# A fused attention and expert layer: peak products in blocks of three, local scores and values in one group, and the norm among the global heads

## The chip, the cores and the metric

The kernel runs on one core of a Trainium2 chip. The time is the device time of one execution in microseconds (us), smaller is better. The engines have short names in the profile: PE is TensorE (PEld its weight loads), DVE is VectorE, ACT is ScalarE, POOL is GpSimd, and SP is SyncE, which issues the DMAs here. Each runs its own queue in order and waits on semaphores.

## The reference

Tokens are 8 sequences of 1024 with 256 features. After a layer norm, two branches are added to the input:

```python
xn = _layernorm(x)                     # over 256 features
# attention: 16 heads of 16, the first 4 global (causal), 12 local (causal, window 64)
scores = einsum('bhqd,bhkd->bhqk', q, k) * 16 ** -0.5
w = softmax(where(mask, -inf, scores)); ctx = einsum('bhqk,bhkd->bhqd', w, v)
attn = ctx @ w_out + b_out
# experts, forward and inverse: 8 experts of rank 64, K side summed over the tokens so far
prod = einsum('btd,kdr->btkr', Q, V) * cumsum(einsum('btd,kdr->btkr', K, W), axis=1)
weights = softmax(gelu(Q @ router_w1.T + b1) @ router_w2.T + b2 + expert_bias)
out = (einsum('btkr,kdr->btd', prod * weights[..., None], U) + weights @ b) / n_valid
x = x + attn + (fwd + alpha * inv) @ W_O.T
```

The kernel works on 512 tokens at a time.

## The kernel before

The 8192 tokens are cut into 16 chunks of 512, two to a sequence. Of a sequence, the first chunk (even number) has few keys before it, and the second (odd number) has all of the first chunk's. One list of stages, written by the planning code at the top of `mixer_layer`, is walked by all five engines: each engine does its own part of a stage and skips the rest. The order of that list is therefore the order of every queue. `weave(main, side)` runs the groups of `main` one by one and puts the groups of `side` evenly between them.

A chunk has three stretches.

1. **Peaks.** Softmax needs the maximum of the scores of every token and head. The products for these maxima are made first: 12 local peaks (`lpeak`, L780, one PSUM bank each, 64-row halves of the PE array) and then the global peaks (`gpeak`, L794, full array), 10 in an even chunk and 26 in an odd one. Each peak fills one of the banks 5, 6 and 7 in turn, and DVE reduces it to a maximum (L1254, L1261). A bank that holds masked scores has to hold the mask first. For the first three local peaks PE writes it (L774), for the other nine, and for the peaks on the diagonal of the global heads, ACT does (`seed`, L1056 and L1058), and PE waits for `seeded`. Between the peaks stand the groups of the experts: `x` (six products of L639 from XH and XL, copied by ACT at L1040, multiplied by a weight on POOL at L1501), `c` (six products of L639 from CH and CL) with `product` (DVE multiplies at L1334, ACT copies the high part to PH at L1050, POOL makes the rest PL at L1506), `mix` (twelve products of L760) and `open` (four products of L727). A chunk has 21 such groups: product 0, c1, open, mix 0, and then x, c, mix in turn.
2. **Local heads.** Six units, each with scores (`lscore`, L814 and L820, exponentials at L1077) and products with the values (`lav`, L841), with the next chunk's transposes (`turn`, L657) and query and key products (`parts`) between them.
3. **Global heads.** Scores (`gscore`, L855), exponentials (L1085), masks on POOL (L1494) and products with the values (`gav`, L873), with the next chunk's router (`gates`, `gate_parts`), then `cout` (PE transposes, DVE divides at L1344 and L1346), `cparts` (L894, L1100, L1353) and `finish` (L904, L1364), which also ends the chunk's output.

The layer norm of a chunk's tokens (`norm`, nine pieces on DVE, L1174 to L1194) is spread over the peaks stretch of the chunk before it. Its tokens are loaded by `load` (L1547) in the local heads' stretch before that.

`peak_groups` gives the peaks in pairs, and it puts the `seed` of a peak behind the peak two places before it, so that on ACT it stands right behind the preceding pair:

```python
        for n, ((stage, *key),) in enumerate(order + gpeaks):
            if stage is add_lpeak and n > 2:
                order[n - 2].append((add_seed, key[-1], "lpeak", *key[:-1]))
```

Of the kernel before, what the change touches and what calls it, by code (L numbers as in the profile page):

```python
# [41 lines left out]
class Plan:  # L42
# [6 lines left out]
    def add(self, kind, *key, uses=()):  # L49
        self.stages.append((kind, *key))  # L50
        self.count[kind] = self.count.get(kind, 0) + 1
        self.place[(kind, *key)] = self.count[kind]
        self.claim((kind, *key), uses)
# [16 lines left out]
def mixer_layer(  # L70
# [4 lines left out]
    KE, _, R = V_fwd.shape  # L75
# [11 lines left out]
    CHUNKS = NB * NC  # L87
# [2 lines left out]
    HALF = C // 2  # L90
    HE_SLOTS = 6
    WIDE = 3
    assert DB == 2 and NC == 2 and KR == 512 and NG == 4 and NL % 4 == 0 and C // WINDOW == 8

    COL_Q, COL_K, COL_V = 0, D, 2 * D
# [17 lines left out]
    add, nth, use = plan.add, plan.nth, plan.use  # L113
# [21 lines left out]
    def peak_use():  # L135
        turns["peak"] += 1
        return f"bank{(5, 6, 7)[turns['peak'] % 3]}"

    NORM = ("moments", "start", "square", "correct", "square", "correct", "square", "correct", "scale")
# [34 lines left out]
    def add_hidden(ch, j):  # L174
        add_on("hidden", ch, j, uses=[f"bank{2 + j % 2}", exp_use()])

    def add_cout(ch, grp):
        add("cout", ch, grp, uses=["bank4", f"craw{grp % 2}"])
# [13 lines left out]
    def add_lav(ch, grp, half):  # L192
        add("lav", ch, grp, half, uses=["bank7"] if half == 0 else [])
        where["lav", ch, grp, half] = [where["lscore", ch, grp, half, pair][1] for pair in range(2)]
        if half == 1:
            add("cin", ch, grp)
# [10 lines left out]
    def weave(main, side):  # L207

        done = 0
        for n, group in enumerate(main):  # L210
            run(group)
            upto = -(-len(side) * (n + 1) // len(main))
            for other in side[done:upto]:
                run(other)
            done = upto

    def run(group):
        for stage, *key in group:
            stage(*key)

    def local_groups(ch):

        units = [(grp, half) for grp in range(1, 1 + NL // 4) for half in range(2)]
        order = []
        for n, (grp, half) in enumerate(units):
            order.append([(add_lscore, ch, grp, half, pair) for pair in range(2)])
            if n:
                order.append([(add_lav, ch, *units[n - 1])])
            if n > 2 and half:
                order[-1].append((add_cout, ch, grp - 1))  # L230
        return order

    def global_groups(ch):
        order = []
        tl = tiles(ch % NC)
        for n, (j, half) in enumerate(tl):
            order.append([(add_gscore, ch, j, half, pair) for pair in range(2)])
            if n:
                order.append([(add_gav, ch, *tl[n - 1])])
        return order + [[(add_gav, ch, *tl[-1])]]  # L240

    def expert_groups(ch):

        order = []
        for j in range(2 * KB):
            if j < 2 * KB - 1 and (j > 1 or not ch):
                order.append([(add_x, ch, j + 1, part) for part in range(2)] + [(add_weigh, ch, j + 1)])
            order.append([(add_c, ch, j, part) for part in range(2)] if j else [])
            order[-1].append((add_product, ch, j))
            if j == 1 and ch:  # L250
                order.append([(add_open, ch)])
            if j:
                order.append([(add_mix, ch, j - 1, part) for part in range(2)])
        return order
# [4 lines left out]
    def add_residual(ch):  # L259
        add("residual", ch)  # L260
# [7 lines left out]
    def add_weigh(ch, j):  # L268

        add("weigh", ch, j)  # L270
        if j + WIDE < 2 * KB:
            add_wide(ch, j + WIDE)

    def add_wide(ch, j):
        add("wide", ch, j, uses=[f"wide{j % WIDE}"])

    def add_gate_parts(ch):
        add("gate_parts", ch)
        for j in range(WIDE):
            add_wide(ch, j)  # L280
# [4 lines left out]
    def add_rows(ch, which):  # L285
        add("rows", ch, which, uses=["bank4"])

    def peak_groups(ch):
        c = ch % NC
        order = [[(add_lpeak, ch, t, grp, peak_use())] for t in range(T) for grp in range(NL // 4)]  # L290
        gpeaks = [[(add_gpeak, ch, t, j, peak_use())] for t in range(T) for j in range(c * T + t + 1)]
        for n, ((stage, *key),) in enumerate(order + gpeaks):
            if stage is add_lpeak and n > 2:
                order[n - 2].append((add_seed, key[-1], "lpeak", *key[:-1]))
            elif stage is add_gpeak and key[2] == c * T + key[1]:
                (order + gpeaks)[n - 2].append((add_seed, key[-1], "gpeak", *key[:-1]))
        order[-1].append((add, "found", ch, 0))
        gpeaks[2].append((add_rows, ch, 0))
        gpeaks[-1].append((add, "found", ch, 1))
        order += gpeaks  # L300
        if ch + 1 < CHUNKS:
            at_ = len(order) // 3
            step = (len(order) - at_) // len(NORM)
            for n in range(len(NORM)):
                order[at_ + n * step].append((add, "norm", ch + 1, n))
        return [order[n] + (order[n + 1] if n + 1 < len(order) else []) for n in range(0, len(order), 2)]


    add("boot")
# [54 lines left out]
    for ch in range(CHUNKS):  # L364
        nxt = ch + 1 < CHUNKS

        experts, peaks = expert_groups(ch), peak_groups(ch)
        split = len(experts) if nxt else 18
        weave(experts[:split], peaks)
        if ch:  # L370
            add_residual(ch)

        last_mix = [(add_mix, ch, 2 * KB - 1, part) for part in range(2)]
        if nxt:
            side = [[(add_turn, ch + 1, 0)], last_mix, [(add_turn, ch + 1, 1)], [(add, "sums", ch + 1, 0), (add_rows, ch, 1)]]
            side += [[(add_parts, ch + 1, 1, 0), (add, "sums", ch + 1, 1)]]
            side += [[(add_parts, ch + 1, w, b)] for w, b in ((1, 1), (0, 0), (0, 1))]
            if ch + 2 < CHUNKS:
                side[-1].append((add, "load", ch + 2))
        else:  # L380
            side = [[(add_rows, ch, 1)]] + experts[split:] + [last_mix]
        weave(local_groups(ch), side)
        add_lav(ch, NL // 4, 1)
        if nxt:
            add("keep", ch + 1)
            add("stacks", ch + 1, "local")
            add_hidden(ch + 1, 0)
            add_hidden(ch + 1, 1)
        add_cout(ch, NL // 4)
        if nxt:  # L390
            add_hidden(ch + 1, 2)
            add_hidden(ch + 1, 3)

        order = global_groups(ch)
        side = []
        if nxt:
            first_x, first_c = ([(add, ch + 1, 0, part) for part in range(2)] for add in (add_x, add_c))
            run(first_x + order[0] + first_c)
            add("logits", ch + 1, uses=["bank7", "craw0"])
            order = order[1:]  # L400
            side = [[(add_gates, ch + 1)], [(add_gate_parts, ch + 1)]] + [[]] * (2 * (ch % NC))
            side += [[(add_values, ch + 1, 0)], [(add_values, ch + 1, 1)]]
        weave(order, side)
        if nxt:
            add("stacks", ch + 1, "global")
            add("weight_rows", ch + 1, uses=["bank7"])
        add_cout(ch, 0)
        if nxt:
            add_weigh(ch + 1, 0)
            run([(add_x, ch + 1, 1, part) for part in range(2)])  # L410
            add_weigh(ch + 1, 1)
        for k in range(DB):
            add_on("cparts", ch, k, uses=[score_use()])
        if nxt:
            run([(add_x, ch + 1, 2, part) for part in range(2)])
            add_weigh(ch + 1, 2)
        add_finish(ch)

    ctx = ExitStack()
    with ctx:  # L420
# [136 lines left out]
        weights_turned, weights_out, weighed = (sem(n) for n in ("weights_turned", "weights_out", "weighed"))  # L557
        wide_in = [sem(f"wide{i}_in") for i in range(WIDE)]
        lpeaks_ps, gpeaks_ps, lscores_ps, gscores_ps, ctx_turned, ctx_hi, out_ps = (
# [887 lines left out]
        def gpsimd_program(e):  # L1447
# [6 lines left out]
            for stage in plan.stages:  # L1454
# [42 lines left out]
                elif kind == "weigh":  # L1497
                    ch, j = key
                    q.wait_ge(bank_read[2], use("bank2", "x", ch, j, 0))
                    q.wait_ge(wide_in[j % WIDE], 16 * 2 * use(f"wide{j % WIDE}", "wide", ch, j))  # L1500
                    e.tensor_tensor(prod[:, j % 3, :], prod[:, j % 3, :], wide[j % WIDE], ALU.mult).then_inc(weighed)  # L1501
# [181 lines left out]
```

## Time and profile before

| | |
|---|---|
| time, median of 3 runs | 1560.65 us (1558.54 to 1561.29) |
| time of the profiled execution | 1558.8 us |
| its span | 1557.1 us |
| PE busy | 1468.7 us (94%), 15153 products |
| DVE busy | 882.2 us (57%) |
| ACT busy | 795.6 us (51%) |
| POOL busy | 444.0 us (29%) |

The 1.7 us between the profiled execution's time and its span lie around the span. A matmul row's duration is longer than the distance to the next one, since matmuls are pipelined: 0.40 us is written behind each product of L639, and one starts every 0.23 us. How long a group takes is therefore read from the distance of starts.

### The profile page before, as it was taken

How to read it: one execution, taken by the hardware profiler on the slowest of the kernel's cores; microseconds unless marked ns; L12 is line 12 of the kernel's file. 1: busy time of each engine (PE TensorE's matmuls, PEld its weight loads, DVE VectorE, ACT ScalarE, POOL GpSimd, SP SyncE). 2: the span in 40 equal slices, each digit the busy share in tenths (PEclk: the TensorE clock that was granted, in tenths of full speed). 3: DMA queues.
4: the chain of work that ended last, by engine and by line, in shares of the span. 5: the costliest groups of instructions: out<-in, count | busy, mean ns of one | idle time of the engine just before them, and what ended most of it. 6: DMA issues, size and time to landing. Idle time of an engine off the chain costs nothing.

```text
span 1557.1 us, 36810 instructions
## 1 busy us (share of the span) xinstructions
PE 1468.7 (94%) x15153; PEld 1082.1 (69%) x15153; DVE 882.2 (57%) x1935; ACT 795.6 (51%) x1432; POOL 444.0 (29%) x471
## 2 busy tenths in 40 slices
PE   5999999999999999999999999999999999999997
PEld 4577775867758676676757767576775867667674
DVE  6675672747637484474836567274762748547361
ACT  3446446463554536555374644646356453654534
POOL 1042331414224231332404233141322413133230
PEclk9999999999999999999999999999999999999999
DMA  8423416153241615316052341615325162531610
GB/s 220 83 71 98 122 35 160 50 124 109 77 125 32 171 61 117 99 44 175 31 137 82 100 131 37 149 61 118 115 69 134 32 162 69 115 100 39 167 31 15
DMA packets 153787, 150.56 MB, mean 97 GB/s; under 512 B 28467, under 2 KB 136884, under 8 KB 153572
## 3 DMA queue, kind: packets, MB, share of 16 engines
q1 hardware_dynamic: 153620, 148.22, 36.1%
q8 instruction: 119, 1.95, 0.5%
q14 instruction: 48, 0.39, 0.1%
HBM read 106.98 MB, written 34.87 MB: 91 GB/s over the span
## 4 chain that ended last, share of the span: by engine, by line
PE 74%; DVE 12%; ACT 7%; issue 4%; POOL 1%; DMA 1%; SPq 0%; DVEq 0%; ACTq 0%; POOLq 0%
PE PS L639 33%; PE PS L760 9%; PE PS L841 4%; PE PS L904 3%; PE PS L873 3%; PE PS L794 3%; PE PS L814 3%; PE PS L820 3%; DVE prod L1334 3%; ACT HE L1085 3%; PE PS L855 3%; PE PS L780 2%; PE PS L885 2%; PE PS L959 2%; DVE block_peak L1261 2%
## 5 line engine op out<-in xcount | busy, mean ns | idle before, releaser
L1506 POOL TENSOR_TENSOR PL<-prod,PH 128x512 fp32r<-128x512 f32 x128 | 164.1, 1282 | 264.7 <-ACT PH L1050 264.2
L639 PE MATMUL PS<-XH,WH 128*128 128x512 f32 x512 | 220.5, 431 | 4.4 <-DVE XL L1201 1.9
L1050 ACT ACTIVATE PH<-prod 128x512 fp32r<-128x512 f32 x128 | 80.9, 632 | 264.0 <-DVE prod L1334 264.0
L639 PE MATMUL PS<-XH,WL 128*128 128x512 f32 x512 | 203.8, 398 | 0.0
L639 PE MATMUL PS<-XL,WH 128*128 128x512 f32 x512 | 203.4, 397 | 0.0
L1261 DVE TENSOR_REDUCE block_peak<-PS 128x4 f32<-128x512 f32 x288 | 188.8, 683 | 8.6 <-PE PS L794 8.6
L1501 POOL TENSOR_TENSOR prod<-prod,rest 128x512 f32<-128x512 f32 x96 | 123.6, 1289 | 243.4 <-ACT prod L1040 144.8
L1494 POOL TENSOR_SCALAR_AFFINE_SELECT HE<-HE 128x256 f32<-128x256 f32 x128 | 50.7, 409 | 478.5 <-ACT HE L1085 475.9
L1085 ACT ACTIVATE HE<-PS 128x512 f32<-128x512 f32 (+1 forms) x320 | 159.7, 552 | 24.9 <-PE PS L855 22.6
L1254 DVE TENSOR_REDUCE peak<-PS 128x4 f32<-128x512 f32 x192 | 124.6, 683 | 35.8 <-PE PS L780 35.5
L1040 ACT ACTIVATE prod<-PS 128x512 f32<-128x512 f32 x128 | 76.2, 595 | 131.2 <-PE PS L639 131.2
L760 PE MATMUL PS<-UH,PH 128*128 128x256 f32 x512 | 135.4, 299 | 0.0
L1344 DVE RECIPROCAL cinv<-PS 128x16 f32<-128x16 f32 x64 | 16.3, 254 | 199.6 <-PE PS L885 199.6
L1334 DVE TENSOR_TENSOR prod<-PS,prod 128x512 f32<-128x512 f32 x128 | 88.1, 688 | 70.2 <-PE PS L639 66.6
L760 PE MATMUL PS<-UL,PH 128*128 128x256 f32 x512 | 125.5, 279 | 0.0
L1077 ACT ACTIVATE HE<-PS 128x512 f32<-128x512 f32 x192 | 103.8, 596 | 23.0 <-PE PS L820 23.0
L639 PEld LDWEIGHTS PS<-XH,WH 128*128 128x128 f32 x512 | 97.0, 189 | 26.4 <-DVE WL L1399 2.2
L639 PEld LDWEIGHTS PS<-XH,WL 128*128 128x128 f32 x512 | 96.9, 189 | 23.1
L639 PE MATMUL PS<-CH,WH 128*128 128x512 f32 x256 | 109.2, 427 | 2.8 <-DVE prod L1334 0.8
L639 PEld LDWEIGHTS PS<-XL,WH 128*128 128x128 f32 x512 | 97.4, 190 | 14.6
L855 PE MATMUL PS<-area 99*128 99x256 bf16 (+1 forms) x640 | 99.6, 265 | 8.1 <-ACT HE L1085 3.9
L855 PEld LDWEIGHTS PS<-area 99*128 99x128 bf16 x640 | 41.4, 97 | 93.0 <-ACT HE L1085 55.8
(193 smaller groups left out, 3163.5 us busy)
## 6 DMA issues: line engine op xcount, KB each, us to landing
parts_d<-area SPq DMA_DIRECT2D x32, 768.0 KB, 5.1
area<-parts_d SPq DMA_DIRECT2D x128, 192.0 KB, 8.4
rest<-weights_d SPq DMA_DIRECT2D x192, 128.0 KB, 2.9
area<-parts_d SPq DMA_DIRECT2D x32, 576.0 KB, 8.5
tok<-in_L_attn_x_dram SPq DMA_DIRECT2D x16, 512.0 KB, 6.3
xt<-in_L_attn_x_dram SPq DMA_DIRECT2D x16, 512.0 KB, 4.0
wide<-weights_d SPq DMA_DIRECT2D x64, 128.0 KB, 3.0
out_dram<-xt SPq DMA_DIRECT2D x16, 512.0 KB, 3.7
```

The source lines that it names most:

```text
L639: ins = e.matmul(ps, a, b, start=first and k == 0, stop=last and k == n - 1, skip_group_check=True)
L760: ins = e.matmul(out_half(t), (PH, PL)[part][:, h, t * P:(t + 1) * P], u[:, j, :], start=False, stop=False, skip_group_check=True)
L855: ins = e.matmul(psum(i, lo=HALF * a + lo, hi=HALF * (a + 1)), KG[0:KSTK, g, j * P:(j + 1) * P], QS[0:KSTK, g, half * HALF + lo:(half + 1) ...
L1040: e.activation(prod[:, j % 3, :], psum(2), ACT.Copy).then_inc(bank_read[2])
L1050: e.activation(PH[:, h, :], prod[:, j % 3, :], ACT.Copy).then_inc(phi)
L1077: e.activation(HE[:, k, :], psum(i), ACT.Exp, scale=SCALE).then_inc(bank_read[i])
L1085: e.activation(two(HE[:, k, :], lo), two(psum(i), lo), ACT.Exp, scale=SCALE).then_inc(bank_read[i])
L1254: e.tensor_reduce(peak[:, t, NG + 4 * grp:NG + 4 * (grp + 1)], psum(i).rearrange("p (a k) -> p a k", a=4), AX_X, ALU.max).then_inc(bank_re ...
L1261: e.tensor_reduce(block_peak[ch % NC][:, t, :, j], psum(i).rearrange("p (a k) -> p a k", a=4), AX_X, ALU.max).then_inc(bank_read[i])
L1334: e.tensor_tensor(prod[:, r, :], psum(3), prod[:, r, :], ALU.mult).then_inc(bank_read[3])
L1501: e.tensor_tensor(prod[:, j % 3, :], prod[:, j % 3, :], wide[j % WIDE], ALU.mult).then_inc(weighed)
L1506: e.tensor_tensor(PL[:, j % 2, :], prod[:, j % 3, :], PH[:, j % 2, :].bitcast(F32), ALU.subtract).then_inc(plo)
```

## The change

Three things, and all only in the order of the list of stages.

- Peaks are run in blocks of three (`PEAKS`), by a new `weave_peaks`. The masks (`seed`) that ACT lays for a block are put behind the expert group that follows the block before, so behind that group's own ACT work.
- In `local_groups`, the product with the values of the preceding unit stands in the same group as the scores of a unit, with no other group between.
- The norm is spread over the global heads' stretch of the chunk two before (`add_norm`). Only chunk 1's stays among the peaks of chunk 0.

```diff
+    PEAKS = 3
...
+    def weave_peaks(main, peaks):
+
+        done, masks = 0, []
+        for n, group in enumerate(main):
+            run(group + masks)
+            masks = []
+            upto = -(-len(peaks) * (n + 1) // len(main))
+            for m in range(done, upto):
+                run(masks + peaks[m][1])
+                masks = peaks[m + 1][0] if m + 1 < len(peaks) else []
+            done = upto
...
             order.append([(add_lscore, ch, grp, half, pair) for pair in range(2)])
             if n:
-                order.append([(add_lav, ch, *units[n - 1])])
+                order[-1].append((add_lav, ch, *units[n - 1]))
...
+    def add_norm(ch, order):
+
+        at_ = len(order) // 3
+        for n in range(len(NORM)):
+            order[at_ + n * (len(order) - at_) // len(NORM)].append((add, "norm", ch, n))
...
+        masks = [[] for _ in order + gpeaks]
         for n, ((stage, *key),) in enumerate(order + gpeaks):
             if stage is add_lpeak and n > 2:
-                order[n - 2].append((add_seed, key[-1], "lpeak", *key[:-1]))
+                masks[n].append((add_seed, key[-1], "lpeak", *key[:-1]))
             elif stage is add_gpeak and key[2] == c * T + key[1]:
-                (order + gpeaks)[n - 2].append((add_seed, key[-1], "gpeak", *key[:-1]))
+                masks[n].append((add_seed, key[-1], "gpeak", *key[:-1]))
...
-        if ch + 1 < CHUNKS:
-            at_ = len(order) // 3
-            step = (len(order) - at_) // len(NORM)
-            for n in range(len(NORM)):
-                order[at_ + n * step].append((add, "norm", ch + 1, n))
-        return [order[n] + (order[n + 1] if n + 1 < len(order) else []) for n in range(0, len(order), 2)]
+        if ch == 0:
+            add_norm(1, order)
+        join = lambda groups: [stage for group in groups for stage in group]
+        return [(join(masks[n:n + PEAKS]), join(order[n:n + PEAKS])) for n in range(0, len(order), PEAKS)]
...
-        weave(experts[:split], peaks)
+        weave_peaks(experts[:split], peaks)
...
             order = order[1:]
+            if ch + 2 < CHUNKS:
+                add_norm(ch + 2, order)
```

What moves is seen best in the queues. In the engines' programs every line number of the kernel after is higher by 20, as the planning code grew: L659 is what L639 was, L780 what L760 was, L800 what L780 was.

PE's queue at the start of an odd chunk, before: masks and local peaks (L774, L780), the group c1 (L639), two peaks, `open` (L727), two peaks.

```order
L774 MATMUL PS<-peak_mask_l,ident_b 128x512
L780 MATMUL PS<-area 64x128 x8
L639 MATMUL PS<-CH,WH 128x512
L639 MATMUL PS<-CL,WH 128x512
L639 MATMUL PS<-CH,WL 128x512
L639 MATMUL PS<-CH,WH 128x512
L639 MATMUL PS<-CL,WH 128x512
L639 MATMUL PS<-CH,WL 128x512
L774 MATMUL PS<-peak_mask_l,ident_b 128x512
L780 MATMUL PS<-area 64x128 x16
L727 MATMUL PS<-bias_rows,WT 128x256 x4
L780 MATMUL PS<-area 64x128 x16
```

The same place in the kernel after (L794 is now the mask, L800 the local peak, L659 the expert product, L747 `open`).

```order
L794 MATMUL PS<-peak_mask_l,ident_b 128x512
L800 MATMUL PS<-area 64x128 x8
L659 MATMUL PS<-CH,WH 128x512
L659 MATMUL PS<-CL,WH 128x512
L659 MATMUL PS<-CH,WL 128x512
L659 MATMUL PS<-CH,WH 128x512
L659 MATMUL PS<-CL,WH 128x512
L659 MATMUL PS<-CH,WL 128x512
L800 MATMUL PS<-area 64x128 x24
L747 MATMUL PS<-bias_rows,WT 128x256 x4
```

All three peaks with a mask of PE's own now stand ahead of c1, and behind c1 stand three peaks (24 products) whose masks come from ACT; before, the first of the two peaks behind c1 had PE's own mask.

ACT's queue in the same stretch, before: the copies of x (L1040), PH (L1050) and the masks (L1056).

```order
L1040 ACTIVATE prod<-PS 128x512
L1050 ACTIVATE PH<-prod 128x512
L1056 ACTIVATE PS<-peak_mask_l 128x512
L1050 ACTIVATE PH<-prod 128x512
L1056 ACTIVATE PS<-peak_mask_l 128x512 x6
L1040 ACTIVATE prod<-PS 128x512
L1056 ACTIVATE PS<-peak_mask_l 128x512 x2
L1050 ACTIVATE PH<-prod 128x512
```

And in the kernel after (L1060 is the copy of x, L1070 PH, L1076 the mask).

```order
L1060 ACTIVATE prod<-PS 128x512
L1070 ACTIVATE PH<-prod 128x512 x2
L1076 ACTIVATE PS<-peak_mask_l 128x512 x6
L1060 ACTIVATE prod<-PS 128x512
L1076 ACTIVATE PS<-peak_mask_l 128x512 x3
L1070 ACTIVATE PH<-prod 128x512
```

No mask stands between the PH copies of products 0 and 1 any more, and the masks of the fourth block stand behind the copy of x3 (in even chunks they stand behind PH of product 2).

DVE's queue in the global heads' stretch, before: the end of `gate_parts`, then the division of `cout` (L1344, L1346) and `cparts` (L1353).

```order
L1323 TENSOR_TENSOR gate<-gate,wstack 128x64
L1325 CAST wstack<-gate 128x4x32
L1327 TENSOR_TENSOR wstack<-gate,wstack 128x4x16
L1344 RECIPROCAL cinv<-PS 128x16
L1346 TENSOR_TENSOR ctok<-PS,cinv 128x4x64
L1353 TENSOR_TENSOR PL<-PS,PH 128x512 x2
```

And in the kernel after, where the norm (L1194, before L1174, and on) follows `gate_parts`.

```order
L1343 TENSOR_TENSOR gate<-gate,wstack 128x64
L1345 CAST wstack<-gate 128x4x32
L1347 TENSOR_TENSOR wstack<-gate,wstack 128x4x16
L1194 BN_STATS stats<-tok 128x6 x4
L1197 BN_AGGR mv<-stats 128x2 x4
L1199 TENSOR_SCALAR var<-mv 128x4
L1201 TENSOR_SCALAR var<-var 128x4
```

All of the norm now stands ahead of `cout`'s division on DVE.

## Rows read from the trace of the kernel before

**Rows 1.** The page: span, and the granted clock in 40 slices.

```profile
span 1557.1 us, 36810 instructions
...
PEclk9999999999999999999999999999999999999999
```

**Rows 2.** What PE waited for: us in total, times, longest.

```profile
PE PS L794 <- ACT PS L1058: 11.1, 14, 1.0
```

**Rows 3.** Timeline, odd chunk, local peaks (start, us, engine, operation, idle before).

```profile
541.02 0.39 PE L774 MATMUL PS<-peak_mask_l,ident_b 128*128 128x512 bf16 x1
541.68 0.39 PE L774 MATMUL PS<-peak_mask_l,ident_b 128*128 128x512 bf16 x1
...
542.55 0.50 PE L639 MATMUL PS<-CH,WH 128*128 128x512 f32 x1
...
544.07 0.39 PE L774 MATMUL PS<-peak_mask_l,ident_b 128*128 128x512 bf16 x1
544.33 0.69 DVE L1334 TENSOR_TENSOR prod<-PS,prod 128x512 f32<-128x512 f32 x1 [0.64 <-PE PS L639]
...
545.06 0.63 ACT L1050 ACTIVATE PH<-prod 128x512 fp32r<-128x512 f32 x1 [1.32 <-DVE prod L1334]
545.59 1.62 ACT L1056 ACTIVATE PS<-peak_mask_l 128x512 f32<-128x512 bf16 x3
...
546.23 0.93 PE L780 MATMUL PS<-area 96*64 96x128 bf16 x16 [0.66 <-ACT PS L1056]
...
548.69 0.64 PE L780 MATMUL PS<-area 96*64 96x128 bf16 x16
...
549.26 0.50 PE L639 MATMUL PS<-XH,WH 128*128 128x512 f32 x1
...
550.85 0.64 PE L780 MATMUL PS<-area 96*64 96x128 bf16 x16
550.96 0.60 ACT L1040 ACTIVATE prod<-PS 128x512 f32<-128x512 f32 x1 [0.48 <-PE PS L639]
...
555.09 0.62 PE L794 MATMUL PS<-area 96*128 96x128 bf16 x8
```

**Rows 4.** PE's timeline, even chunk, from the first mask to the first global peak.

```profile
642.22 0.39 PE L774 MATMUL PS<-peak_mask_l,ident_b 128*128 128x512 bf16 x1
...
646.15 0.61 PE L727 MATMUL PS<-bias_rows,WT 99*128 99x256 bf16 x4
646.52 0.36 PE L760 MATMUL PS<-UH,PH 128*128 128x256 f32 x1
...
648.10 0.64 PE L780 MATMUL PS<-area 96*64 96x128 bf16 x16
...
662.27 0.62 PE L794 MATMUL PS<-area 96*128 96x128 bf16 x8
```

**Rows 5.** The chain that ended last, same chunk: start, us, what (two groups in a row).

```profile
648.73 3.00 PE PS L639 x12
```

**Rows 6.** PE's timeline, global peaks of an odd chunk (two rows), first scores of an even one.

```profile
560.49 0.62 PE L794 MATMUL PS<-area 96*128 96x128 bf16 x8 [0.97 <-ACT PS L1058]
...
574.67 0.40 PE L794 MATMUL PS<-area 96*128 96x128 bf16 x4 [0.62 <-ACT PS L1058]
...
678.55 0.38 PE L814 MATMUL PS<-mask_l,ident_b 128*128 128x512 bf16 x1 [0.22 <-DVE block_peak L1261]
```

**Rows 7.** DVE's and PE's timeline, end of an even chunk's global heads.

```profile
534.17 0.26 DVE L1344 RECIPROCAL cinv<-PS 128x16 f32<-128x16 f32 x1 [5.88 <-PE PS L885]
...
535.38 1.03 PE L894 MATMUL PS<-ident,ctok 128*128 128x128 f32 x8
```

**Rows 8.** DVE's timeline, pieces of the norm among the peaks of an odd chunk.

```profile
557.17 1.40 DVE L1174 BATCH_NORM_STATS2 stats<-tok 128x6 f32<-128x256 f32 x4
...
560.50 0.17 DVE L1183 TENSOR_SCALAR var<-var 128x4 int32<-128x4 int32 x1
...
575.37 1.37 DVE L1194 TENSOR_SCALAR tok<-tok,mv,var 128x256 f32<-128x256 f32 x4
```

## The prediction

> **What bounds the kernel now.** The page first: PE is busy nearly everywhere, and its granted clock stands at the upper level (90% of 2.4 GHz or more) in all 40 slices [rows 1]. So the time goes by what PE's queue holds and by how long PE stands. Then the waits: the longest that PE has behind another engine inside the loop is for masks that ACT lays into the peaks' banks, 11.1 us in 14 waits for the global peaks alone [rows 2]. Then the timelines of the peaks stretch of one odd and one even chunk [rows 3, 4], since chunks repeat nearly to the hundredth, and the places where it waits later [rows 6]. In rows 3 the reader is to follow one chain: the last product of c1 ends about 544.07, DVE's product starts 0.26 later, PH another 0.73 later, the masks 0.53 behind PH, and PE's next masked peak 0.64 behind that, at 546.23. From the end of c1 to a peak whose mask stands behind PH it is 2.16 us.
>
> **Lengths of groups, by distances of starts.** Mask and peak by PE: 0.66 (541.02 to 541.68). Two peaks with masks ready: 0.57 (548.69 to 549.26), so three are about 0.80. Three peaks whose masks come one by one: the three masks take 1.62, so they are 0.54 apart, and the block takes 2 x 0.54 + 0.34 = 1.42 [rows 3]. c1: 1.52. x3 between two local blocks: 1.59 [rows 3]; two such groups in a row: 3.00 [rows 5], so 1.40 to 1.41 for one without a block before or behind. I share the difference of 0.19 as 0.10 behind a block and 0.09 ahead of a local one. `open` 0.37, a mix behind it 1.58, so 1.40 bare as well [rows 4].
>
> **Peaks, odd chunk, up to the first global peak.** Before: 541.02 to 555.09, 14.07 [rows 3]. After, walked with the same pieces: three masks and peaks, 541.02 to 543.00. c1 to 544.52 (bank 3, for which c1 before had to wait about 0.2, is free by then). Behind c1 stands a block whose masks are behind PH of product 1, and nothing else for PE to do: it starts at 544.52 + 2.16 = 546.68 and ends at 548.10. `open` and mix 0 to 550.05, a block with masks ready to 550.85. x3 to 552.35. Now the masks stand behind the copy of x3, and the block again follows at once: the copy starts 0.2 after x3 ends (550.96 is 0.11 behind a start that is itself 0.09 late), 552.55; masks 0.50 to 0.53 later, first peak 0.64 behind that, 553.69; block ends 555.11. c2 and mix 1: 558.01. That is 16.99, **2.92 more**. PE stands in it 2.1 + 0.7 at the second block and 1.3 + 0.7 at the fourth; before 0.75 + 0.3 and 0.2. The switches that are saved (six blocks become four) are in the walk already.
>
> **Even chunk.** Before: 642.22 to 662.27 [rows 4]. After: blocks stand behind product 0, `open`, c2 and x4. c1 ends at 645.72, the masked block starts 2.16 later at 647.88, of which `open` covers 0.37, and ends at 649.30. mix 0, x3, c2 to 653.69 (1.50 + 1.40 + 1.49), block to 654.49, mix 1 and x4 to 657.48, block to 658.28 (its masks stand behind PH of product 2, with mix 1 and x4, 3 us, over them), c3, mix 2, x5 to 662.58. c4 (1.40) stood ahead of the first global peak before and still has to be done: 663.98 against 662.27, **1.71 more**.
>
> **Global peaks.** Removed are the waits with idle 0.97 and 0.62 in the odd chunk (1.13 and 0.78 by starts) and one of 0.26 that the idle column does not show; they come since the seeds' banks wait for DVE, which has the norm between its reductions (1.40 at 557.17, [rows 8]). In the even chunk one of about 0.28, and 0.38 at the first scores (idle 0.22) [rows 6]. Masks here stand a group ahead of their block after the change, so I put their waits at nothing: the cover is c or x of 1.40 behind, and without it they would cost about 1.2 each, four an odd chunk. New: where c stands before a block and the next block is one group on, DVE has a product and three reductions (0.69 each at most, the product's row in rows 3) from 0.26 on, so the third bank comes free by 2.4 to 3.0, and PE wants it at 0.65 + 0.09 + 1.40 + 0.43 = 2.57. Twice an odd chunk, 0 to 0.45 each: I take 0.25. Blocks of global peaks: 13 become 9 odd, 5 become 4 even, at 0.08 each. Odd: -2.17 + 0.50 - 0.33 = -2.0. Even: -0.66 - 0.08 = -0.74.
>
> The Trainium skill (TensorEngine Tiling (Array Packing), Key Properties) says that changing the tiling mode drains TensorE. By it alone fewer and longer local blocks gain. The trace agrees in size, 0.09 to 0.12 a switch: a gain of about 0.4 a chunk, in the walk above, which a single wait for a mask outweighs.
>
> **Local heads.** Nothing is added or removed. Three adjacencies a chunk between scores and a float32r group go, and three between scores and values come, each at about 0.1, so between -0.1 and +0.1 a chunk. DVE's last two reductions may hold the first scores of an odd chunk by up to 0.25. I take 0 for both together, with ends of -2 and +3 us in all. The turn products find their tokens ready in either order. On SP the last weight row load now stands behind the local maxima's write and read in odd chunks; its weight is wanted some ten groups on, so I cost it at nothing.
>
> **The norm.** In the peaks it only costs where a seed waits, counted above. Among the global heads DVE has to do it between `gate_parts` and the division of `cout`. In an even chunk DVE is idle there for 5.88 [rows 7]. The norm in one piece is 1.40 + 0.4 + 0.2, 14 small operations of 0.17 at about 0.19 apart (2.7), and 1.37: 6.1 [rows 8]. The division comes 0.2 late, at 534.4, and ends by 535.1; PE reads ctok at 535.38 [rows 7]. So nothing, with 0.3 in hand. But DVE operations that would take 0.2 take about 1.1 in places while POOL works, and POOL masks scores just there. If this adds 1.2 to the norm, each of 7 even chunks pays 0.9: the bounds are 0 and 7 us, and I take 0. In odd chunks there are 14 tiles instead of 6, so it is covered. The tokens are there: they are loaded in the local heads' stretch.
>
> **Sum.** Odd 2.92 - 2.0 = 0.9, even 1.71 - 0.74 = 1.0. Eight of each: 15. On the profiled execution (1558.8, span 1557.1) that makes 1574; the median shown, 1560.65, is 1.9 above that execution, so I say **1575**.
>
> **Rivals.**
> - *The masks' waits are paid back, and the kernel gets faster.* The mechanism: if the second and fourth blocks found their masks as early as before (waits of 1.1 in an odd chunk and 0 in an even one instead of 4.8 and 2.5), the rest of the change would gain: 15 - 8 x 3.7 - 8 x 2.5 = -34, 1526. If half of it, -10, 1551. It decides at 0.9 us a chunk less wait than I walked (15 over 16 chunks). For it: the removed waits (some 1.7 a chunk) are surely gone. Against it: ACT's queue has both PH copies ahead of all masks, and PH cannot start before c1 has ended.
> - *It comes out even*, within 0.2% (3 us, about what a measurement of this kernel can tell from no change): the gains must be 1 us a chunk larger, or the chain shorter by it. 1561.
> - *The norm is the worse half.* It collides with POOL's masks and holds `cout`'s division: 7 us on top, 1582; more if it also delays the masks on which the values wait.
> - *The clock.* New pauses of 1.3 to 2.1 us stand in each chunk. The granted clock is at the upper level throughout, with pauses of at most about 1.1 in the loop [rows 1, 6], so nothing in the rows speaks for a fall. If one group of 1.40 behind each of some 24 long pauses ran at 1.2 GHz, it would cost 34 more, 1609. The Trainium skill (TensorE: Matmul & The Clock Gate, HAM oscillation) tells of kernels whose clock falls in pauses for data.
>
> **How the numbers follow.** My forecast (1567 to 1580) 0.62; norm worse 0.11; clock 0.03; a smaller loss, between 1564 and 1567, 0.04; even 0.08; faster 0.12. Range: from 1562, which leaves out the faster case and part of the even one, to 1584, the forecast with POOL's bound on top. Slower 0.80, same 0.08, faster 0.12.
>
> **What would show it.** Right: PE's idle before L800 behind ACT's masks of 30 to 50 us in all instead of single figures, in every chunk at the second block, in odd ones at the fourth; waits at L814 (global peaks, before L794) down to 1 or 2 us; first mask to first global peak about 17.0 in an odd chunk; L894's turn unchanged in an even one. Wrong: a second block that starts less than 1.5 after c1 ends; an idle column at `cparts` or at `gav` that grew; a slice with a lower clock.

## The result and the profile after

The kernel after takes 1602.23 us, median of 4 runs (1594.74 to 1605.85), against 1560.97 for the kernel before (4 runs, 1558.54 to 1563.03). The ratio is 1.0259, with a 95% interval of 1.0225 to 1.0293: slower by 41 us, where I had said 14. It lies outside the range that I gave.

The page first, of the profiled execution of after (1603.15 us).

```profile
span 1601.4 us, 36810 instructions
...
PE 1488.7 (93%) x15153; PEld 1109.3 (69%) x15153; DVE 860.6 (54%) x1935; ACT 795.5 (50%) x1432; POOL 444.0 (28%) x471
...
PEclk9999999999999999999999999999999999999999
```

The span has grown by 44.3 us. PE has as many products as before, 15153, but is busy for 1488.7 us instead of 1468.7. So 20.0 us of the growth stand as longer work, and 24.3 us as idle time (112.7 instead of 88.4). The line of the granted clock shows nines only, as in [rows 1], and says nothing of the first: one slice is 40 us wide, and a short fall leaves it at 9. The mean clock of the core does say something: 0.979 against 0.997.

The waits of PE, in the columns of [rows 2].

```profile
PE PS L800 <- ACT PS L1076: 39.6, 24, 3.4
...
PE PS L814 <- ACT PS L1078: 3.3, 6, 1.0
...
PE PS L914 <- DVE ctok L1366: 1.9, 8, 0.8
```

The local peaks wait 39.6 us for masks in 24 waits: two in each odd chunk and one in each even one, except that chunk 0 has two and chunk 15 one. For the global peaks 3.3 us are left of the 11.1 in [rows 2].

The timeline of the peaks stretch of one odd chunk, local peaks, start to first global peak. [Rows 3] are its counterpart.

```profile
939.04 0.39 PE L794 MATMUL PS<-peak_mask_l,ident_b 128*128 128x512 bf16 x1
...
941.04 0.50 PE L659 MATMUL PS<-CH,WH 128*128 128x512 f32 x1
...
944.71 1.45 PE L800 MATMUL PS<-area 96*64 96x128 bf16 x24 [2.00 <-ACT PS L1076]
946.09 0.61 PE L747 MATMUL PS<-bias_rows,WT 99*128 99x256 bf16 x4
...
948.03 0.86 PE L800 MATMUL PS<-area 96*64 96x128 bf16 x24
948.82 0.50 PE L659 MATMUL PS<-XH,WH 128*128 128x512 f32 x1
...
951.66 1.45 PE L800 MATMUL PS<-area 96*64 96x128 bf16 x24 [1.18 <-ACT PS L1076]
...
955.96 0.84 PE L814 MATMUL PS<-area 96*128 96x128 bf16 x12
```

The two pauses stand where the walk had them, 2.00 at the second block and 1.18 at the fourth, and the stretch takes 955.96 - 939.04 = 16.92 us, against 16.99 walked. In an even chunk `open` stands in the pause and covers part of it; 1.55 are left, as here in chunk 6.

```profile
666.48 1.45 PE L800 MATMUL PS<-area 96*64 96x128 bf16 x24 [1.55 <-ACT PS L1076]
```

Now the same stretch of another odd chunk.

```profile
556.21 0.39 PE L794 MATMUL PS<-peak_mask_l,ident_b 128*128 128x512 bf16 x1
...
559.98 0.69 DVE L1354 TENSOR_TENSOR prod<-PS,prod 128x512 f32<-128x512 f32 x1 [0.49 <-PE PS L659]
...
560.70 0.63 ACT L1070 ACTIVATE PH<-prod 128x512 fp32r<-128x512 f32 x1 [2.35 <-DVE prod L1354]
561.24 1.62 ACT L1076 ACTIVATE PS<-peak_mask_l 128x512 f32<-128x512 bf16 x3
...
561.88 1.68 PE L800 MATMUL PS<-area 96*64 96x128 bf16 x24 [2.00 <-ACT PS L1076]
563.48 1.03 PE L747 MATMUL PS<-bias_rows,WT 99*128 99x256 bf16 x4
...
564.53 0.41 PE L780 MATMUL PS<-UL,PH 128*128 128x256 f32 x1
564.74 0.41 PE L780 MATMUL PS<-UH,PH 128*128 128x256 f32 x1
...
568.43 0.78 PE L659 MATMUL PS<-XH,WH 128*128 128x512 f32 x1
...
575.84 0.34 PE L814 MATMUL PS<-area 96*128 96x128 bf16 x3
```

The chain is as before up to the mask: DVE's product, PH, masks, peak. From there the same work runs slower. From 563.48 to 568.43, 4.95 us, PE does `open`, mix 0 and three peaks, for which the other chunk takes 2.73 (946.09 to 948.82). The products of a mix start every 0.21 us (564.53 to 564.74). The stretch to the first global peak is 19.63 instead of 16.92.

Windows over both places: length, then busy time of PE, PEld, DVE, ACT and POOL with counts, the granted clock, the DMA share and GB/s. The first three cut the chunk with slow products, the last is the same place in the other.

```profile
560.00:562.10 2.10, 0.22 (x8) 0.23 (x8) 0.67 (x1) 1.40 (x3) 0.69 (x1) 1.00 0.40 124
562.10:568.90 6.80, 6.70 (x65) 5.66 (x60) 3.19 (x6) 2.56 (x5) 0.57 (x1) 0.51 0.53 180
568.90:572.00 3.10, 1.89 (x14) 1.05 (x13) 0.68 (x2) 1.59 (x4) 0.92 (x1) 0.98 0.00 0
...
945.00:951.80 6.80, 5.41 (x72) 4.17 (x68) 3.77 (x6) 3.77 (x8) 1.11 (x2) 1.00 0.51 168
```

For 6.8 us the granted clock is at 0.51, the lower level of 1.2 GHz, ahead of it at 1.00 and behind it at 0.98. It fell right behind the pause at the second block. Such a stretch, 3.4 or 6.8 us long, stands in chunks 0 and 1 (two in each), 2, 5 to 8 and 11 to 15, and in none of 3, 4, 9 and 10, although every chunk has the pause. What it costs shows in the lengths of chunks, from first mask to first mask.

| | odd chunk | even chunk |
|---|---|---|
| before | 101.2 | 84.1 |
| after, clock held | 101.9 | 85.4 |
| after, clock fell | 104.4 to 104.6 | 86.9 |
| forecast for after | 102.1 | 85.1 |

The four runs of after fit that: mean clocks of 0.986, 0.980, 0.979 and 0.978 go with 1594.74, 1601.31, 1603.15 and 1605.85 us. The higher the mean clock, the shorter the time.

Chunk 0 is a place of its own: it costs 7 us more (chunk 1 starts at 177.5 instead of 170.4), with these two waits and two falls.

```profile
89.53 1.45 PE L800 MATMUL PS<-area 96*64 96x128 bf16 x24 [3.35 <-ACT PS L1076]
...
103.23 1.45 PE L800 MATMUL PS<-area 96*64 96x128 bf16 x24 [1.11 <-ACT PS L1076]
```

### The profile page after: what moved, and what is told of

The parts are those of the page before. It is cut to its first block, busy times and chain, and to the rows that moved or that the text cites. A ratio compares the mean times of both kernels' runs of the same rounds, so it can differ in the third digit from the quotient of the medians.

```text
span 1601.4 us, 36810 instructions
## 1 busy us (share of the span) xinstructions
PE 1488.7 (93%) x15153; PEld 1109.3 (69%) x15153; DVE 860.6 (54%) x1935; ACT 795.5 (50%) x1432; POOL 444.0 (28%) x471
## 4 chain that ended last, share of the span: by engine, by line
PE 78%; DVE 10%; ACT 7%; issue 3%; POOL 1%; DMA 1%; SPq 0%; ACTq 0%; DVEq 0%; POOLq 0%
PE PS L659 33%; PE PS L780 11%; PE PS L814 4%; PE PS L861 3%; PE PS L800 3%; PE PS L924 3%; PE PS L840 3%; PE PS L834 3%; PE PS L893 3%; PE PS L875 2%; ACT HE L1105 2%; ACT PS L1076 2%; PE PS L905 2%; PE PS L979 2%; DVE PL L1373 1%
## 5 line engine op out<-in xcount | busy, mean ns | idle before, releaser
L1070 ACT ACTIVATE PH<-prod 128x512 fp32r<-128x512 f32 x128 | 80.8, 631 | 298.6 <-DVE prod L1354 298.6
L659 PE MATMUL PS<-XH,WH 128*128 128x512 f32 x512 | 218.9, 428 | 4.5 <-DVE XL L1221 1.9
L1281 DVE TENSOR_REDUCE block_peak<-PS 128x4 f32<-128x512 f32 x288 | 180.5, 684 | 61.7 <-PE PS L814 61.7
L659 PE MATMUL PS<-XL,WH 128*128 128x512 f32 x512 | 204.1, 399 | 0.0
L659 PE MATMUL PS<-XH,WL 128*128 128x512 f32 x512 | 202.9, 396 | 0.0
L1060 ACT ACTIVATE prod<-PS 128x512 f32<-128x512 f32 x128 | 76.0, 594 | 195.6 <-PE PS L659 195.6
L1274 DVE TENSOR_REDUCE peak<-PS 128x4 f32<-128x512 f32 x192 | 121.0, 683 | 84.9 <-PE PS L800 84.8
L780 PE MATMUL PS<-UH,PH 128*128 128x256 f32 x512 | 141.8, 308 | 0.0
L780 PE MATMUL PS<-UL,PH 128*128 128x256 f32 x512 | 134.1, 292 | 0.0
L659 PEld LDWEIGHTS PS<-XH,WH 128*128 128x128 f32 x512 | 98.0, 191 | 27.1 <-issue 3.1
L800 PE MATMUL PS<-area 96*64 96x128 bf16 x1536 | 75.9, 238 | 43.5 <-ACT PS L1076 39.6
L659 PEld LDWEIGHTS PS<-XH,WL 128*128 128x128 f32 x512 | 97.3, 190 | 23.7
L659 PE MATMUL PS<-CH,WH 128*128 128x512 f32 x256 | 109.5, 428 | 0.6 <-DVE prod L1354 0.6
L659 PEld LDWEIGHTS PS<-XL,WH 128*128 128x128 f32 x512 | 98.2, 192 | 14.8
L780 PEld LDWEIGHTS PS<-UH,PH 128*128 128x128 f32 x512 | 103.6, 202 | 4.5 <-issue 0.2
```

The source lines that it names most:

```text
L659: ins = e.matmul(ps, a, b, start=first and k == 0, stop=last and k == n - 1, skip_group_check=True)
L780: ins = e.matmul(out_half(t), (PH, PL)[part][:, h, t * P:(t + 1) * P], u[:, j, :], start=False, stop=False, skip_group_check=True)
L800: ins = e.matmul(PS[64 * w:64 * (w + 1), i, P * a:P * (a + 1)], QS[0:G16, NG + l, q0:q0 + WINDOW], KL[0:G16, l, q0:q0 + P], start=False, s ...
L1070: e.activation(PH[:, h, :], prod[:, j % 3, :], ACT.Copy).then_inc(phi)
L1274: e.tensor_reduce(peak[:, t, NG + 4 * grp:NG + 4 * (grp + 1)], psum(i).rearrange("p (a k) -> p a k", a=4), AX_X, ALU.max).then_inc(bank_re ...
L1281: e.tensor_reduce(block_peak[ch % NC][:, t, :, j], psum(i).rearrange("p (a k) -> p a k", a=4), AX_X, ALU.max).then_inc(bank_read[i])
```

## The experiments

The theory after the result: the loss comes wholly from masks that ACT lays late in the blocks of three, partly as waits and partly as TensorE's clock, which falls behind the longest of these waits; the rest of the change gains. Its rivals: the norm, now beside POOL's masks in the global heads, costs; blocks of three cost by themselves (a drain, banks that come free late); or the clock falls for a reason that has nothing to do with the pauses. The kernel before was run beside each group of kernels, with medians of 1561.61, 1561.16 and 1561.49 us.

**All masks early (e1_masks_early).** Masks of a block go right behind the block before it, ahead of the next expert group's ACT work. This holds for all blocks, those of the global peaks included. Nothing else changes.

```diff
-            run(group + masks)
-            masks = []
+            run(group)
...
-                run(masks + peaks[m][1])
-                masks = peaks[m + 1][0] if m + 1 < len(peaks) else []
+                run(peaks[m][1])
+                if m + 1 < len(peaks):
+                    run(peaks[m + 1][0])
```

> The kernel after, with one thing undone: ACT lays the masks of a block right behind the block before it, ahead of the next expert group's own ACT work. Theory A (the loss is PE standing for masks behind PH, and the clock that falls in those pauses): both go, the gains of blocks and norm stay, 1530 us (1522 to 1540), granted clock 0.995 or more, PE's wait for ACT's local masks under 8 us. Theory B (the norm among the global heads is what costs): the time stays above 1560 us.

Measured: 1525.74 us (1524.79 to 1530.77), ratio 0.9782 [0.9758, 0.9806]. Its waits for masks:

```profile
PE PS L814 <- ACT PS L1078: 1.6, 4, 0.7
PE PS L800 <- ACT PS L1076: 1.1, 3, 0.7
```

And the second block of an odd chunk, on the timeline:

```profile
533.55 0.63 ACT L1070 ACTIVATE PH<-prod 128x512 fp32r<-128x512 f32 x1 [4.02 <-DVE prod L1354]
...
534.15 1.79 ACT L1076 ACTIVATE PS<-peak_mask_l 128x512 f32<-128x512 bf16 x3
...
535.62 0.86 PE L800 MATMUL PS<-area 96*64 96x128 bf16 x24
...
536.52 0.63 ACT L1070 ACTIVATE PH<-prod 128x512 fp32r<-128x512 f32 x1 [0.58 <-DVE prod L1354]
```

The masks now stand between the PH copies of products 0 and 1 and run while PE is in c1; the block follows c1 with no idle time and takes 0.86 instead of 1.45. The mean clock is 0.996, and no stretch at the lower level stands in any chunk's peaks; the short ones ahead of chunk 0 and behind the last scores are in the kernel before too. The three waits for local masks (0.75 the longest) are all in chunk 15. The position of the masks alone turns 41 us of loss into 36 of gain, 77 us together. This kernel beats both. It rules out that the moved norm, the blocks of three and the join, taken together, cost anything, and without the long pauses the falls among the peaks are gone too.

**Which block counts (e5_second_early, e6_fourth_early).** Of the kernel after, only the masks of the second local block are early, or only those of the fourth (there with 3 in place of 1).

```diff
                 run(masks + peaks[m][1])
                 masks = peaks[m + 1][0] if m + 1 < len(peaks) else []
+                if m + 1 == 1:
+                    run(masks)
+                    masks = []
```

> The kernel after, with the masks of the second block alone laid right behind the first block. Theory A (each late block costs its pause, and the clock falls behind the second block's): even chunks as in the run with all masks early, 83 us, odd ones 97.5 + 1.9 (the fourth block's pause as walked) = 99.4, no fall of the clock in the loop, together about 1541 us (1534 to 1548). If the fourth block's pauses alone make the clock fall too, odd chunks of 101 us and more, and 1552 us.

Measured: 1549.81 (5 runs, 1543.60 to 1554.76), 0.9932 [0.9904, 0.996]. The chunks came out as expected where the clock held, 99.4 and 83.2. The median is 9 us above the expectation and outside its range, close to the 1552 of the rival (the fourth block's pauses make the clock fall too). Three of the odd chunks of the profiled run have a fall of 3.4 us behind the fourth block: chunks 1 and 13, behind a pause of 1.18 (they take 100.9), and chunk 15, where the pause is only 0.75. And chunk 0 keeps most of its loss (chunk 1 starts at 174.7). The runs differ: the shortest run has a mean clock of 0.997, the two longest 0.988. The waits that are left, and the fourth block of the first odd chunk on PE's timeline:

```profile
PE PS L803 <- ACT PS L1079: 10.5, 11, 1.2
```

```profile
184.86 1.45 PE L803 MATMUL PS<-area 96*64 96x128 bf16 x24 [1.18 <-ACT PS L1079]
```

The fourth block of chunk 15, and a window behind it:

```profile
1461.20 0.41 PE L803 MATMUL PS<-area 96*64 96x128 bf16 x8 [0.75 <-ACT PS L1079]
```

```profile
1463.80:1467.10 3.30, 3.30 (x12) 2.52 (x10) 0.00 (x0) 0.38 (x1) 0.00 (x0) 0.50 0.19 67
```

Two more waits of 0.18 follow that of 0.75, between the peaks of the block. The kernels e7 and e10 below have the same waits and a fall behind them in chunk 15; e1 has them and its clock stays at 1.00 there. So no length of pause by itself decides whether the clock falls.

> The kernel after, with the masks of the fourth block alone laid right behind the third. In even chunks nothing stood for it, so they stay (85.4 us, 86.9 with a fall); odd ones lose the fourth pause: 101.9 - 1.9 = 100.0 without a fall. Theory A: the falls stay, as they begin behind the second block: 1585 us (1578 to 1592). If the fall needs both pauses, odd chunks of 100.0 us throughout, and 1575 us or less.

Measured: 1583.90 (1583.12 to 1585.92), 1.0148 [1.0133, 1.0163], as expected. The chunks have 12 falls, one of them in chunk 0, each of 3.4 us and none of 6.8. Its waits, then the second block of an odd chunk on PE's timeline, then windows around it:

```profile
PE PS L803 <- ACT PS L1079: 30.1, 17, 3.1
```

```profile
182.27 1.45 PE L803 MATMUL PS<-area 96*64 96x128 bf16 x24 [2.00 <-ACT PS L1079]
```

```profile
181.00:184.00 3.00, 1.52 (x28) 1.07 (x29) 1.34 (x4) 2.70 (x5) 1.27 (x1) 1.00 0.46 144
184.00:187.40 3.40, 3.40 (x31) 3.17 (x30) 0.72 (x3) 1.25 (x3) 0.00 (x0) 0.55 0.82 267
187.40:191.00 3.60, 3.60 (x47) 2.77 (x44) 2.81 (x5) 2.31 (x4) 0.60 (x1) 0.95 0.05 17
```

The pause of 2.00 is still there, the clock falls 2.0 us after its end (at 184.3, as the share of 0.55 in the window from 184.0 tells), and is back 3.4 later. So from 1602 the second block's masks are worth 52 us and the fourth's 18. All masks early (e1) are worth 77, some 6 more than the sum of the two; e1 also has the masks of the global peaks early, and no run separates that part. The fall behind the second block's pause often lasts 6.8 us in after; here, without the fourth block's pause that follows, it is always 3.4.

**Waits kept, clock held (e9_lean_filler, e2_filler).** To split waits and clock, useless mask products into a bank that nobody reads keep PE busy while it would wait; nothing of the computation is left out. In e9 five at the second block's first peak, and three at the fourth's in odd chunks:

```diff
+                        place = 3 * t + grp
+                        for _ in range({3: 5}.get(place, 0) + ({9: 3}.get(place, 0) if ch % NC else 0)):
+                            e.matmul(psum(4).rearrange("p (a k) -> p a k", a=4), ident_b[:, :], local_peak_mask(ch, t),
+                                     start=True, stop=True, skip_group_check=True)
```

> As the filler run, with less filling, so that none of it can lengthen a chain: 5 products of no use before the first peak of the second block and, in odd chunks, 3 before that of the fourth, none between the masks. In the chunks of the kernel after in which the clock did not fall, 101.9 and 85.4 us. If the clock is held by this much too, chunks of 101.9 and 85.4 us throughout and 1583 us (1578 to 1588), which would make the fillers' own cost in the earlier run 0.3 to 0.5 a chunk. If less filling does not hold the clock, falls return and the time lies between 1590 and 1602 us.

Measured: 1582.32 (1581.14 to 1583.83), 1.0126 [1.0109, 1.0143], as expected. On the timeline, the fillers and the peaks behind them; a window over that place; and the waits that are left:

```profile
284.29 1.24 PE L793 MATMUL PS<-peak_mask_l,ident_b 128*128 128x512 bf16 x5
286.00 1.45 PE L804 MATMUL PS<-area 96*64 96x128 bf16 x24 [0.47 <-ACT PS L1080]
```

```profile
283.00:291.00 8.00, 7.33 (x59) 5.24 (x58) 3.19 (x6) 4.45 (x8) 2.12 (x2) 1.00 0.13 46
```

```profile
PE PS L804 <- ACT PS L1080: 17.5, 25, 2.1
```

In this even chunk the fillers take 1.24 us and 0.47 of the pause stays idle; in an odd one 0.91 of 2.00 and 0.5 of 1.18 stay. The block starts no earlier and no later than in after: chunks of 101.8 to 101.9 and 85.3 us, those of after with the clock held. But the clock stays up behind it, in every chunk from 1 on (the two falls of chunk 0 remain, the first behind 2.05 us that stay idle there). The kernel thus waits as long as after does and is 19.9 us shorter. **So the clock's falls in the loop cost 20 us of the 41, and the waits, less what the rest gains, 21** (chunk 0's two falls are among the latter). Against e1, e9 is 57 us longer: that is what the waits and chunk 0 cost, and the 36 by which e1 beats the kernel before are what the rest gains. This also shows what makes the clock fall: it is PE's standing, since nothing else was altered.

e2 was the first attempt, with seven fillers at the first peak and one at each of the next two (four, one and one at the fourth block).

> The kernel after, with products of no use put where PE stands: masks of 512 columns written into bank 4, which nobody uses then; 7 before the first peak of the second block, 1 before each other one, and in odd chunks 4, 1 and 1 at the fourth block (12.5 on average a chunk, some 0.22 us each, no longer than the pauses walked). The chain to the masks is as before. Theory A, whose two parts this tells apart: the pauses stay (now filled), the clock does not fall, so the time goes from 1602 to about 1577 (1572 to 1584), the clock to 0.995 or more. Theory C (the clock's share is small and the waits are longer than walked): 1598 us or more.

Measured: 1590.93 (1589.65 to 1595.28), 1.0197 [1.0179, 1.0216]; no falls from chunk 1 on, but chunks of 102.4 and 85.7 and a wait of 8.5 us in 18 pieces. The expectation was missed by 14 us, and its range too (the fillers are 12 a chunk on average, not the 12.5 written there): a filler between two peaks puts them 0.67 apart instead of 0.52, so the fillers themselves delayed PE by 0.55 an odd and 0.35 an even chunk, chunk 0 and the last chunk cost 8 and 5 more than before, and I had hoped that chunk 0 would lose its falls too. It says the same of the clock, less cleanly.

**The parts alone (e3_norm_only, e4_local_only).** The kernel before, with only the norm moved:

```diff
-        if ch + 1 < CHUNKS:
-            at_ = len(order) // 3
-            step = (len(order) - at_) // len(NORM)
...
+        if ch == 0:
+            add_norm(1, order)
...
+            if ch + 2 < CHUNKS:
+                add_norm(ch + 2, order)
```

> The kernel before with the norm alone moved among the global heads. Theory A: the global masks' waits, 11.1 us, and some 5 us at the first scores and elsewhere shrink, nothing is added at the output's transposes: 1548 us (1540 to 1555). Theory B (the norm holds up the division of cout): 1562 us or more, with a wait of PE at the transposes of ctok.

Measured: 1546.83 (1545.41 to 1549.33), 0.9912 [0.9897, 0.9927]. Chunks of 99.4 and 84.1. The 11.1 us of [rows 2] are gone from the list of waits; what is left there behind ACT's masks is

```profile
PE PS L788 <- ACT PS L1064: 6.2, 9, 0.9
```

The local peaks' own waits are what they were (6.2 us in 9 in the kernel before as well). The gain is 1.8 us an odd chunk and nothing in an even one. In the profiled run chunk 0 loses 2.8, by a wait of 1.9 for DVE's product with a fall of the clock behind it.

And before with only the values' products joined to the next unit's scores:

```diff
             if n:
-                order.append([(add_lav, ch, *units[n - 1])])
+                order[-1].append((add_lav, ch, *units[n - 1]))
```

> The kernel before with the local heads' groups alone joined. Theory A: as many switches as before, 1560 us (1557 to 1563). If the join is worth something of its own, 1555 us or less; if it holds PE at a bank, above 1565 us.

Measured: 1558.12 (10 runs, 1556.85 to 1559.44), 0.9982 [0.9973, 0.9991], chunks of 101.0 and 83.9: a gain of 3.5 us (with an interval of 1.4 to 4.2 by the ratio), 0.2 a chunk.

**The parts taken from the best kernel (e7, e8, e10).** Each is e1 with one part undone. In e7_early_norm_in_peaks the norm is back among the peaks. It is not placed as in the kernel before: there its pieces stood one or two peaks apart, here `add_norm` spreads them to the end of the peaks.

```diff
-        if ch == 0:
-            add_norm(1, order)
+        if ch + 1 < CHUNKS:
+            add_norm(ch + 1, order)
...
-            if ch + 2 < CHUNKS:
-                add_norm(ch + 2, order)
```

> The run with all masks early, with the norm put back among the peaks. The norm's own move gave 14.8 us to the kernel before, nearly all in odd chunks (99.4 instead of 101.2). If it is worth the same with blocks of three: 1540 us (1535 to 1545). If blocks of three leave DVE enough room, 1530 us or less.

Measured: 1545.46 (1543.51 to 1549.28), 0.9903 [0.9885, 0.9921], chunks of 97.9 and 85.3: the norm's place is worth 19.7 us here, 5 more than on the kernel before and than expected. Nearly all of it is in the even chunks, 2.3 us each, where moving the norm gained nothing on the kernel before; the odd ones lose 0.4. In each even chunk from 2 on PE waits 1.0 for DVE's product and 0.85 for local masks, which it does not in e1:

```profile
PE PS L657 <- DVE prod L1352: 8.6, 9, 1.1
...
PE PS L798 <- ACT PS L1074: 7.1, 10, 0.9
```

Whether the blocks of three or the wider spread of the norm's pieces bring these waits is not shown; no run has blocks of three with the norm spread as before.

In e8_early_pairs the blocks are of two.

```diff
-    PEAKS = 3
+    PEAKS = 2
```

> The run with all masks early, with PEAKS = 2. It is then close to the kernel before with the norm and the local heads' change together: 1543 us (1539 to 1548) if the gains add up. The difference to 1525.7 us is what threes are worth: by switches 0.5 a chunk I would have 8 us, so 1534 us; if more, threes also take waits away.

Measured: 1548.88 (1547.37 to 1550.36), 0.9922 [0.9907, 0.9936], chunks of 99.2 and 84.0: just outside the range that was expected. Threes are worth 23 us, where I had expected 17. Part of it is in waits that threes do not have:

```profile
PE PS L800 <- ACT PS L1076: 6.2, 9, 0.9
PE PS L834 <- DVE block_peak L1281: 5.5, 9, 2.5
```

The mask waits are 5.1 us less with threes (1.1 in e1), and the 5.5 at the first scores fall away. The other 12 us fit fewer blocks: at 0.19 to 0.21 for the switch in and out of a local block, and 0.08 for a global one, the 2 local and 4 or 1 global blocks saved come to about 0.7 an odd and 0.5 an even chunk, or 10 in all. This sum is an argument; no run separates the switch from the wait.

In e10_early_local_apart the values' products have their own group again.

```diff
-                order[-1].append((add_lav, ch, *units[n - 1]))
+                order.append([(add_lav, ch, *units[n - 1])])
```

> The run with all masks early, with the local heads' groups as before (scores and values apart). The join gave 3.5 us alone. If it is worth the same here: 1529 us (1527 to 1532). If the longer gap between blocks and scores mattered only with the norm gone, 1535 us or more.

Measured: 1530.60 (1529.21 to 1532.61), 0.9798 [0.9784, 0.9813], chunks of 97.7 and 83.2: the join is worth 4.9 us, within what was expected.

## Why the prediction was wrong

The sign and the place were right, and the size of the waits; the time was not. By its own steps:

- **The failing step is the clock.** I wrote that "nothing in the rows speaks for a fall", since the kernel before has pauses of up to 1.1 us in the loop and a clock at the upper level, and gave the rival a chance of 0.03. That reading went from pauses of 1.1 to pauses of 2.0, for which the trace had no row; it should have stayed open, with its price inside the range. The rival's shape was nearly right: a slow stretch behind the long pauses, 12 of them from chunk 1 on instead of 24, each costing 1.5 us (even chunk) or 2.6 (odd), together 20 by e9 (5 x 1.5 + 6 x 2.6 = 23 by the profiled run's chunks) instead of the 34 that I had put. The forecast plus that is 1595, the lower end of what the runs of after show. The page that the prediction named beside this rival, the Trainium skill, TensorE: Matmul & The Clock Gate, tells in its section "A second HAM failure mode: psum-queue depth-cycling" of a kernel in which TensorE stops briefly between groups of products, often enough that its clock goes back and forth between the two levels. The windows of after agree in kind, 0.51 behind a pause of 2.00, in 11 of the 15 chunks behind chunk 0.
- **The order of the masks.** Right. From the start of c1 to the masked peak 3.68 us were walked (1.52 for c1, 2.16 for the chain); it took 3.67 (941.04 to 944.71). First mask to first global peak 16.99 against 16.92. PE's idle time before the local peaks, forecast as 30 to 50 us, is 39.6.
- **Odd and even chunks.** +0.9 and +1.0 forecast; +0.7 and +1.25 measured where the clock held. The waits for the global peaks' masks went from 11.1 to 3.3, where the forecast had 1 or 2; 1.0 of that is in chunk 0.
- **Chunk 0 was mis-sized.** I counted it as any even chunk, +1.0, though the stretch of c and product is slower there. It costs 7: a wait of 3.35 where the other even chunks have 1.55, a second of 1.11 which they don't have, and two falls. That is the other 6 us.
- **The norm in even chunks.** Costed at nothing, with 7 as a bound. The timeline of after, DVE from the norm to the division, and POOL's masks:

```profile
543.08 1.40 DVE L1194 BATCH_NORM_STATS2 stats<-tok 128x6 f32<-128x256 f32 x4
...
544.61 1.66 POOL L1514 TENSOR_SCALAR_AFFINE_SELECT HE<-HE 128x256 f32<-128x256 f32 x4 [3.42 <-ACT HE L1105]
...
545.56 0.33 DVE L1203 TENSOR_SCALAR var<-var 128x4 int32<-128x4 int32 x1
...
548.50 1.39 DVE L1214 TENSOR_SCALAR tok<-tok,mv,var 128x256 f32<-128x256 f32 x4
549.80 0.25 DVE L1364 RECIPROCAL cinv<-PS 128x16 f32<-128x16 f32 x1
```

  It takes 6.7 us instead of the 6.1 walked, as three operations that run beside POOL's masks take 0.33 to 0.40, where one of them took 0.17 in [rows 8]. PE then waits for ctok for 1.9 us in 8 waits, 1.1 more than the 0.8 of the kernel before. The cover held.
- **The rival that gains.** "If the masks were as early as before" gave 1526. The kernel e1, which does just that, takes 1525.74. The agreement is partly luck: by 0.4 a chunk in local blocks and 0.08 for each global one I had the switches at some 10 us, and threes are worth 23; but the join, which I put at nothing, gains 3.5 to 5, and e1 still has 0.996 of a full clock and 2.7 us of mask waits.

## What to carry to other kernels

Where a helper engine prepares a buffer for another engine, its place in the helper's queue is part of the change: put behind work that itself waits for the engine served, it makes a wait of the whole chain (here 2.16 us), and put one group earlier it costs next to nothing (1602 against 1526 us with the same instructions). A pause of TensorE is to be priced twice, once for its length and once, as a bound, for the clock behind it. That holds above all when it is longer than any that the trace shows to be harmless, but pauses that did no harm in one run did in another, as in chunk 15. Useless products in the pause tell the two apart in one run. And the page's clock line, with slices of 40 us, cannot show falls of 3 to 7: read windows, or compare the distance of starts.

## What the runs showed of the hardware

- The granted clock fell to 1.2 GHz (0.51 and 0.55 in windows) behind pauses of 2.0 us in odd and 1.55 us in even chunks, which are followed by two short ones between the masked peaks (three peaks take 1.45 us instead of 0.86), in a kernel that is 93% busy. It did so in 11 of the 15 chunks behind chunk 0 and not in the other 4, with the same order. The fall began at the end of the pause in chunk 7 of after (753.4) and 2.0 us after it in chunk 1 of e6, and lasted 3.4 or 6.8 us. Behind pauses of 1.18 it happened in 2 odd chunks of e5, and in chunk 15 behind one of 0.75 in e5, e7 and e10, but not in e1.
- Five useless products, 1.24 us together, in the second block's pause, and three in the fourth's, kept the clock up in every chunk of e9 from 1 on.
- Blocks of three peaks instead of two, with the masks in time, were worth 23 us, more than the switches' own 10 or so.
